# Causal maxima of two heads as row-split pairs, in an attention and mixture-of-experts layer

## What is computed

```python
scores = jnp.einsum('bhid,bhjd->bhij', q, k) / jnp.sqrt(hd)
std_out = out_proj(jax.nn.softmax(jnp.where(mask, scores, neg), axis=-1))
gsa_scores = scores + position_sensitivity * splat_attn
gsa_out = out_proj(jax.nn.softmax(jnp.where(mask, gsa_scores, neg), axis=-1))
attn = (1.0 - blend) * std_out + blend * gsa_out
```

## Time and profile before

| | us |
|---|---|
| runs of the kernel | 376.22, 376.65, 376.99 |
| the profiled execution, whole | 378.75 |
| its span | 376.9 |

### The profile page before, as it was taken

The page is one execution under the profiler, slowest core; times in us unless marked ns, Lnnn a source line. Parts: engine busy times, 40 slices in busy tenths (PEclk is TensorE's granted clock), DMA queues, the critical chain, the costliest instruction groups (busy, mean ns, idle before and its releaser), DMA issues.

```text
span 376.9 us, 6181 instructions
## 1 busy us (share of the span) xinstructions
PE 334.7 (89%) x2172; PEld 174.8 (46%) x2172; DVE 230.7 (61%) x614; ACT 194.1 (51%) x278; POOL 65.7 (17%) x82
## 2 busy tenths in 40 slices
PE   0999996788979999999999999999999999989965
PEld 0643663343345544554455445544554454335433
DVE  4555857587674665567556655766577558776222
ACT  1699824525414365436543654366346547767530
POOL 7200140400047530110111011102010007710000
PEclk9999768598979999999999999999999999999995
DMA  6408623304341354245655565547555525510011
GB/s 220 131 0 103 107 38 41 60 13 60 47 135 15 41 75 73 71 89 102 142 153 105 113 139 153 107 93 154 129 125 111 79 53 127 143 42 2 0 57 56
DMA packets 27330, 33.01 MB, mean 88 GB/s; under 512 B 6593, under 2 KB 20097, under 8 KB 27297
## 3 DMA queue, kind: packets, MB, share of 16 engines
q1 hardware_dynamic: 23745, 28.32, 37.4%
q0 software_dynamic: 2128, 4.22, 3.9%
q10 hardware_dynamic: 1424, 0.04, 0.2%
HBM read 15.60 MB, written 4.28 MB: 53 GB/s over the span
## 4 chain that ended last, share of the span: by engine, by line
PE 72%; DVE 14%; ACT 9%; issue 3%; DMA 1%; SPq 0%; DVEq 0%; ACTq 0%
PE ps L817 16%; PE ps L745 9%; PE ps L800 8%; PE ps L788 7%; PE ps L754 7%; PE ps L718 6%; ACT arena_p L636 6%; DVE mx L1093 5%; PE ps L676 4%; PE ps L773 2%; PE ps L695 2%; PE ps L758 2%; PE ps L791 2%; DMA acc<-in_x_dram 1%; ACT small L641 1%
## 5 line engine op out<-in xcount | busy, mean ns | idle before, releaser
L636 ACT ACTIVATE arena_p<-ps 128x1024 f32<-128x1024 f32 (+1 forms) x192 | 147.2, 811 | 79.4 <-PE ps L800 53.7
L1093 DVE TENSOR_REDUCE mx<-ps 128x1 f32<-128x512 f32 (+3 forms) x160 | 89.3, 590 | 33.2 <-PE ps L718 22.7
L817 PE MATMUL ps<-arena_p,v_full 128*32 128x512 f32 (+3 forms) x768 | 72.6, 496 | 0.6 <-ACT arena_p L636 0.6
L718 PE MATMUL ps<-stage 96*128 96x512 bf16 (+3 forms) x160 | 51.5, 362 | 7.1 <-DVE mx L1093 4.7
L788 PE MATMUL ps<-stage 98*128 98x512 bf16 (+1 forms) x192 | 51.9, 337 | 4.7 <-ACT arena_p L636 4.2
L800 PE MATMUL ps<-stage 98*128 98x512 bf16 (+1 forms) x192 | 47.4, 332 | 3.0 <-ACT arena_p L636 2.4
L641 ACT ACTIVATE small<-ps 128x176 f32<-128x176 f32 x24 | 7.6, 318 | 64.1 <-PE ps L745 64.1
L387 POOL DMA_INDIRECT wt<-xn_scratch,ids_sb x16 | 15.2, 951 | 133.2 <-PE ps L735 127.6
L817 PEld LDWEIGHTS ps<-arena_p,v_full 128*32 128x32 f32 x768 | 20.2, 110 | 35.4 <-issue 30.3
L754 PE MATMUL ps<-arena_o,small 88*128 88x256 f32 x96 | 27.4, 409 | 8.3 <-DVE small L1116 6.3
L788 PEld LDWEIGHTS ps<-stage 98*128 98x128 bf16 x192 | 18.8, 100 | 23.5 <-ACT arena_p L636 9.8
(11 more groups left out here) (193 smaller groups left out, 418.5 us busy)
## 6 DMA issues: line engine op xcount, KB each, us to landing
w_sb<-in_w_dram SPq DMA_DIRECT2D x16, 352.0 KB
stage<-split SPq DMA_DIRECT2D x48, 96.0 KB, 2.9
stage<-split SPq DMA_DIRECT2D x48, 64.0 KB, 2.7
arena_o<-in_w_dram SPq DMA_DIRECT2D x16, 176.0 KB
stage<-split SPq DMA_DIRECT2D x80, 32.0 KB, 2.5
ye_scratch<-wt SPq DMA_DIRECT2D x16, 128.0 KB, 1.8
stage<-split SPq DMA_DIRECT2D x32, 48.0 KB
acc<-in_x_dram SPq DMA_DIRECT2D x2, 512.0 KB, 4.6
```

The costliest lines, as they stand in the source:

```text
L636: A(to, ps[:, 1 + 2 * s:3 + 2 * s, off:CH], ACT.Exp, scale=SCALE).then_inc(done, 1)
L718: ins = M(b[:, 0:n1 - n0], lhs, ks[0:KR, pr, h, n0:n1], start=True, stop=not diag)
L817: ins = M(ps[c:c + 2 * HD, 0, off:CH], v_full[:, jb + s, g * GH + h, :], of, start=jb + s == 0, stop=end)
L1093: V.reduce_max(mx[:, it // TC, h, it % TC, pc:pc + 1], b[:, 0:n1 - n0], AX.X).then_inc(aux_free, 1)
```

## The change

- q's and k's rows get another order. Head 0: rows 0 to 31 and 32 to 63 hold parts 0 and 1 of q against parts 0 and 1 of k (four products), rows 64 to 95 the other two, ones and shift rows at 96 and 97. Head 1: the four products in rows 64 to 127, the other two in 32 to 63, shift rows at 0 and 1, and zeros in rows 2 to 31. The scores use rows 0 to 97 and 0 to 127.
- A maximum is taken from the four products alone (64 rows). Both heads' matmuls of a block are issued one after the other, head 0 in rows 0 to 63 and head 1 in rows 64 to 127, into two banks; the masks follow. TensorE waits for the second of the two banks at the start.
- The lists of maxima go by block and then head, and both heads of a block get the same slot. In groups 2 and on that makes pairs in slots 1, 2, 5, 7, 9, 10, 11, 14, 15, 17 and 18 (slot 1 has `max2`, that is two pairs); in group 0, for group 1, slots 5, 6, 7 and one pair in each of 10, 11, 13, 14, 15, 17, 18, 19.
- q and k rows take 16 issues a group instead of 12 (same bytes); the ones take six issues for `ks` and one for `fk`, instead of one each. In group g the 16 are spread over the same twelve slots.
- GpSimd clears rows 0 to 31 of head 1 in `qs` and `ks`, ahead of the clearing of the feature rows; SyncE waits for that before its ones.

```diff
-    stage = [sb(f"stage{n}", [KS, QB if n < 2 else 2, GH, T], bf16) for n in range(4)]
+    QK_RUNS = [[(0, 0, 0, 2), (32, 1, 0, 2), (64, 0, 2, 1), (80, 2, 0, 1)],
+               [(64, 0, 0, 2), (96, 1, 0, 2), (32, 0, 2, 1), (48, 2, 0, 1)]]
+    QK_ALL = [slice(0, KS), slice(0, 128)]
+    QK_TOP = [slice(0, 64), slice(64, 128)]
+    QK_SHIFT = [slice(KR, KS), slice(0, 2)]
+    stage = [sb(f"stage{n}", [P, QB, GH, T] if n < 2 else [KS, 2, GH, T], bf16) for n in range(4)]
...
-        max0 = [("max2", (h,)) for h in range(GH)] + [("max", (h, it, 0)) for h in range(GH) for it in range(2, TC)]
-        max1 = [("max", (h, it, pc)) for h in range(GH) for it in range(TC, NT) for pc in range(2)]
+        max0 = [("max2", (h,)) for h in range(GH)] + [("max", (h, it, 0)) for it in range(2, TC) for h in range(GH)]
+        max1 = [("max", (h, it, pc)) for it in range(TC, NT) for pc in range(2) for h in range(GH)]
...
-            return [(late[len(late) * n // len(tasks)], t) for n, t in enumerate(tasks)]
+            return [(late[len(late) * (n // GH * GH) // len(tasks)], t) for n, t in enumerate(tasks)]
...
-        N_QK, N_F = 12, 19
+        N_QK, N_F = 16, 19
+        ROWS_QK = [(n, h) + run for n in range(2) for h in range(GH) for run in QK_RUNS[h]]
...
+            for t in (qs, ks):
+                nc.gpsimd.memset(t[0:32, :, 1, :], 0.0).then_inc(rows_clear, 1)
...
+            sp.wait_ge(rows_clear, 2)
             sp.wait_ge(ones_set, 2)
-            for t in (ks, fk):
-                sp.dma_start(t[KR:KS, :, :, :].rearrange("p r h t -> p (r h t)"), ones_b[0:t.shape[1] * 32, :]).then_inc(ones_in, 16)
+            for h in range(GH):
+                for b in range(QB):
+                    sp.dma_start(ks[QK_SHIFT[h], b, h, :], ones_b[0:16, :]).then_inc(ones_in, 16)
+            sp.dma_start(fk[KR:KS, :, :, :].rearrange("p r h t -> p (r h t)"), ones_b[0:64, :]).then_inc(ones_in, 16)
...
-                        load_qk_row(sp, g + 2, (g + 2) % QB, at - 10, qk_in[(g + 2) % QB])
+                        for j in range(N_QK * (at - 10) // 12, N_QK * (at - 9) // 12 if at < 22 else 0):
+                            load_qk_row(sp, g + 2, (g + 2) % QB, j, qk_in[(g + 2) % QB])
...
+            def maxima_of_heads(g, t, pr):
+                kind, a = t
+                places = [place(g, (kind, (h,) + a[1:])) for h in range(GH)]
+                if places[1][1] > AB:
+                    pe.wait_ge(aux_free, places[1][1] - AB)
+                blocks = [(0, 0, P, 0), (1, 0, 2 * P, P)] if kind == "max2" else [(a[1], a[2] * CH, min((a[1] + 1) * P, (a[2] + 1) * CH), 0)]
+                for it, n0, n1, at in blocks:
+                    diag, last = n1 == (it + 1) * P, it == blocks[-1][0]
+                    for h in range(GH):
+                        rows, b = QK_TOP[h], ps[:, places[h][0], :]
+                        ins = M(b[:, at:at + n1 - n0], qs[rows, pr, h, it * P:(it + 1) * P], ks[rows, pr, h, n0:n1],
+                                start=True, stop=not diag)
+                        if last and not diag:
+                            ins.then_inc(aux_full, 1)
+                    for h in range(GH if diag else 0):
+                        end = at + n1 - n0
+                        ins = M(ps[:, places[h][0], end - P:end], ident_b[:, :], mask_n[:, :], start=False, stop=True)
+                        if last:
+                            ins.then_inc(aux_full, 1)
...
-                    ins = M(b[:, off:CH], ks[:, pr, h, (jb + s) * P:(jb + s + 1) * P],
-                            qs[:, pr, h, ic * CH + off:(ic + 1) * CH], start=True, stop=not diag)
+                    rows = QK_ALL[h]
+                    ins = M(b[:, off:CH], ks[rows, pr, h, (jb + s) * P:(jb + s + 1) * P],
+                            qs[rows, pr, h, ic * CH + off:(ic + 1) * CH], start=True, stop=not diag)
```

More of the change, by code:

```diff
@@ L299, in shape_of @@
             return off, jb // TC == ic
-        N_QK, N_F = 12, 19
+        N_QK, N_F = 16, 19
+        ROWS_QK = [(n, h) + run for n in range(2) for h in range(GH) for run in QK_RUNS[h]]
         def load_qk_row(eng, g, b, j, done):
-            n, h = j // 6, j % 6 // 3
-            row, part, num = RUNS[j % 3]
+            n, h, row, part, first, num = ROWS_QK[j]
             head = g * GH + h
             m, p0 = head * HD // P, head * HD % P
-            src = split[p0:p0 + HD, 0, part:part + 1, m, :].to_broadcast((HD, num, T)) if n == 0 else split[p0:p0 + HD, 1, 0:num, m, :]
+            src = split[p0:p0 + HD, 0, part:part + 1, m, :].to_broadcast((HD, num, T)) if n == 0 else split[p0:p0 + HD, 1, first:first + num, m, :]
             eng.dma_start(stage[n][row:row + num * HD, b, h, :], src).then_inc(done, 16)
@@ L456, in _ @@
             sp.wait_ge(zeros_out, 16)
-            sp.wait_ge(ones_in, 32)
+            sp.wait_ge(ones_in, 16 * (GH * QB + 1))
             needed = sp.value_load(wide[0:1, 0:1], min_val=0, max_val=1)
@@ L516, in _ @@
                             load_feature_row(sp, g + 1, (g + 1) % 2, j, f_in[(g + 1) % 2])
-                    if g + 2 < NG and 0 <= at - 10 < N_QK:
+                    if g + 2 < NG and at >= 10:
                         if at == 10 and g == 1:
@@ L701, in aux @@
                 if kind == "add" or (kind == "route" and a != CUM):
+                    return
+                if kind in ("max2", "max"):
+                    if a[0] == 0:
+                        maxima_of_heads(g, t, pr)
                     return
@@ L706, in aux @@
                     pe.wait_ge(aux_free, count - AB)
-                if kind == "max2":
-                    for it in range(2):
-                        n0, n1 = it * P, it * 2 * P + P
-                        M(b[:, n0:n1], qs[0:KR, pr, a[0], it * P:(it + 1) * P], ks[0:KR, pr, a[0], 0:(it + 1) * P],
-                          start=True, stop=False)
-                        ins = M(b[:, n1 - P:n1], ident_b[:, :], mask_n[:, :], start=False, stop=True)
-                elif kind == "max":
-                    h, it, pc = a
-                    n0, n1 = pc * CH, min((it + 1) * P, (pc + 1) * CH)
-                    diag = n1 == (it + 1) * P
-                    lhs = qs[0:KR, pr, h, it * P:(it + 1) * P]
-                    ins = M(b[:, 0:n1 - n0], lhs, ks[0:KR, pr, h, n0:n1], start=True, stop=not diag)
-                    if diag:
-                        ins = M(b[:, n1 - n0 - P:n1 - n0], ident_b[:, :], mask_n[:, :], start=False, stop=True)
-                elif kind == "shift":
+                if kind == "shift":
                     pe.wait_ge(mhl_ready, (g + 1) * NC + (a + 1))
@@ L829, in _ @@
             needed = pe.value_load(wide[0:1, 0:1], min_val=0, max_val=1)
+            OWN = [slice(0, KR), QK_ALL[1]]
             with pe.If(needed > 0):
@@ L866, in _ @@
             pe.wait_ge(v_done, NT // 2)
-            pe.wait_ge(ones_in, 32)
+            pe.wait_ge(ones_in, 16 * (GH * QB + 1))
             std(0, 0, 0)
```

9 lines of the change are left out of this document (5 added, 4 removed).

## The result

The changed kernel takes 406.03 us (median; 401.23 to 409.53), the kernel before 376.82 beside it (376.22 to 377.81). Ratio 1.068, 95% interval 1.061 to 1.074. The direction was forecast, the size was not: +25.6 us (+29.2 by the medians) instead of +11.9.

What follows compares the result with a forecast made beforehand. TensorE's matmuls and waits were taken to bound a steady group. Start 4.7, group 0 0.4, groups 1 to 5 6.6 and group 6 0.2 made +11.9 on 376.65: 388.5 us, range 375 to 394.

Steps and rivals of the forecast that it cites:

- C = 0.23: Array-shape switches around each pair: 0.10 us in, 0.03 lag of the second half, 0.10 out; bounds 0 and 0.30.
- Rivals 1: The array takes 64-row pairs with no loss: 376.2 us with the start's delay (chance 0.12), 371.5 without (0.08).
- rival 3: The two halves of a pair run in series, 1.8 us more in seven groups: 401 us, chance 0.05.
- The order, +1.3 a group: Steady group with both heads' maxima in one slot, walked in seven terms: +1.3 us each, +6.6 in groups 1 to 5.
- C, D: Slot 7: 640 columns and a mask become a pair of 512, +0.11 us; slots 9, 10: y's wait goes, -0.38.
- E, F and G's y: Slots 11 to 15: +0.01 and -0.15 us; slots 17, 18: a second reduction delays y from 225.11 to about 225.9.
- A: Slots 0 to 2, up to the gate-up matmul: three pairs, and slot 3's hidden maximum moves to slot 2, +0.40 us.
- B: Slots 5 and 6: reductions of both heads ahead of the hT copy that y awaits, +0.79 us.
- The start, +4.7: Eight more SyncE issues ahead of group 0's feature rows delay the first splat by 4.7 us; bounds 0 and 5.4.
- Rival 2: SyncE's delay at the start does not show, but the array-shape switches do: 383.8 us, chance 0.12.
- Steady SyncE issues, 0: Steady groups: four more issues (2.5 us) fall into SyncE's pauses before y's stores and cost 0.
- Group 0, +0.4 and group 6, +0.2: Group 0: only slot 7's change acts, +0.4 us; group 6: earlier last reduction, +0.2; bounds -1.2 and +2 each.

Runs made afterwards that it cites:

- run with late rows of group 1: Changed kernel with group 1's q and k loads issued behind the shared expert's weights: 430.98 us beside 411.57, ratio 1.050.
- second profile: The changed kernel, unchanged, run and profiled again: 403.46 us beside 376.96, ratio 1.071.
- experts first: Expert's steps put ahead of the maxima within a slot: changed kernel 389.47 us, ratio 1.032; kernel before 368.09 beside 377.36, ratio 0.976 (fourth run).
- order alone: Kernel before with only the new order, slots and pair code, full array, 96 rows, old loads: 392.28 us beside 377.55, ratio 1.035.
- earlier issues: Changed kernel with its 16 q and k loads issued two a slot from slot 10: 401.51 us, ratio 1.060.

## Why the prediction was wrong, step by step

**What bounds the kernel: held.** TensorE's matmuls and waits, in its order of work, set the steady group.

**Pairs, C = 0.23: held.** 0.22 measured, 0.11 on either side; the halves start 3 to 6 ns apart, so the 0.03 taken for a lag isn't there and the two ends are a little dearer. Rivals 1 and 3 fall with it: that rival 3's 401 us is near the measured time is chance. The Trainium skill (TensorE: Matmul & The Clock Gate, Measured speedup vs the span model) gives a pack of tiles no price at its ends; the rows say 0.11 us each. The Trainium skill (TensorEngine Tiling (Array Packing), Key Properties) says that a change of tiling mode drains the engine, and the rows agree.

**The order, +1.3 a group: mis-sized in two of seven terms.** At full clock group 2 of the run with late rows of group 1 is +2.35 (40.51 against 38.16, group 3 of before, by the ends of the groups). The anchors are the y matmuls, counted from the start of the group, before and then in that full-clock group: slot 6 at 7.96 and 10.51 (+2.55), slot 10 at 15.18 and 17.26 (+2.08), slot 18 at 29.19 and 31.89 (+2.70), slot 22 at 35.20 and 37.57 (+2.37). From slot 6 to slot 10 the forecast had -0.27 (C, D) and it is -0.47; to slot 18, 0.65 (E, F and G's y) against 0.62; behind it -0.27 against -0.33. All of the error is ahead of slot 6, where A and B were to be +1.19. Up to the gate-up matmul (197.51 - 195.78 = 1.73 in before, 179.68 - 176.97 = 2.71 after) it is +0.98 and not A's +0.40: the third pair waits 0.42 us for a bank, since it asks for two of three. B is +1.57 and not +0.79: 0.51 us of waiting for a bank, which I had mentioned and not priced, and 0.5 us for the three operations on the negated maxima.

**The clock: the step that was missing.** Every term was priced at 2.4 GHz, because the profile of before shows 1.00 in its steady groups. Nowhere did the prediction ask what a longer wait does to it. Groups 1 to 5 are +27.6 us in the profiled execution. Its falls are four of 6.8 us and one of 3.4; at 3.0 and 1.5 us each (estimates from groups 2 and 5, above) they make 13.7, and the other 13.9 are the order with its late rows. In the second profile groups 1 to 5 are +21.7 us, one long and three short falls, 7.5 us, and 14.2 the rest. So in the faster runs the order is the larger part, 14 us where 6.6 were forecast, and the clock the second, where nothing was. That the fall needs the idleness is shown from two sides: taking the wait away (experts first) and filling it (the added matmuls) each bring the clock to 1.00 in all steady groups. The number was there to be had: group 0 of before, slices as above, with a clock of 0.86 over the group.

**The start, +4.7: 3.7.** The mechanism held; the move of group 1's rows took it back. The issues themselves last 5.3 us more (to 48.64 instead of 43.30), nearer the mean's 5.4 than the median's 4.7; SyncE is 5.9 us later at the first issue behind the flag, 4.9 at the first L332 (64.22; 59.29 in before), and the splat 3.7, so pauses behind the flag gave part of it back. Rival 2 falls.

**Steady SyncE issues, 0: wrong in kind, small in size.** The last six of the 16 stand behind the y store of slot 18 (issued at 246.58, when VectorE's copy is done), and group 3's and 4's first pairs wait 0.8 and 0.4 us for them. The order alone, with the old 12 loads, has such waits too (0.20 and 0.64 us in the same groups), so it is y's later store as much as the four more issues. With experts first or earlier issues the wait is gone.

**Group 0, +0.4 and group 6, +0.2:** -1.2 and +1.5. Within the bounds given. Group 6 is 27.7 us with the order alone too, so it is the order's and not the split's; by which wait wasn't followed. GpSimd's clearing and the xn write stayed hidden (the write left at 16.32, as forecast), and the standard scores on 128 rows cost nothing that shows.

So of the 31.7 us between the first two profiles about 14 are the order with the late rows, 13.7 the clock, 2.5 the start with group 0 and 1.5 group 6; of the 26.9 us between the second two, 14.2, 7.5, 3.9 and 1.3. The steps that failed are the price of the order ahead of slot 6, A and B, and the clock, which had no term. The split into row halves costs nothing at full clock: its overlap (1.92 us of columns a group) pays for its switches and no more. Whether it adds falls of the clock is open.

## What to carry to other kernels

Two row halves side by side save the columns of one, and cost 0.2 us to enter and leave: by these numbers a stretch breaks even near 530 columns (an estimate, 0.22 us at 2.4 GHz), and single pairs scattered between full-height work gain nothing. Before a change that puts waits on TensorE, look in the profile for a place where it already waits and the granted clock is lower behind it: the wait can cost itself plus the half speed after it, here 1.08 us and another 1.5 or 3.0. Ask of each slot what the next engine's queue holds ahead of the one copy on which TensorE's next step depends; to put that step's producer first was worth 13 us in the changed kernel and 9.3 us (2.4%) in the one before.

## What the runs showed of the hardware

Added matmuls made a kernel 4.0 us faster (ratio 1.068 to 1.056), by filling a wait of about 1 us of TensorE. The granted clock fell to 0.50 at the same place in two different kernels, behind y's wait in slot 6, and in 7 of 20 groups it didn't, with the same wait. It stayed low for 3.4 us or for 6.8 in the same kernel, with TensorE busy nearly throughout; why not equally long isn't settled. A 64-row matmul costs 0.10 us on either side even if it is alone.

In half of the sets of experiments groups 0 and 6 hold stalls that no change of the kernel moved. From the chain of waits of one such run (experts first in the kernel before), in order of time, start and length:

```profile
318.33 12.71 another core or an unknown queue
...
331.06 0.60 ACT arena_p L636
331.66 5.71 another core or an unknown queue
```

The same kernel in the other kind of set has no such piece and ends 33 us earlier. What ScalarE waited for is open.
